# VectorE's order of work in the group loops of a graph network: the sums of a finished group are added ahead of the newest group's moments and roots

## What is computed

```
def _mlp(h, W1, b1, W2, b2, g, beta):
    h = silu(h @ W1 + b1)
    h = silu(h @ W2 + b2)
    return g * (h - mean(h)) * rsqrt(var(h) + 1e-5) + beta

edge_attr = _mlp(edge_attr, emb_...)                      # the embedding, edge_attr has 3 columns
for l in range(2):                                        # the two edge layers
    msg_in = concatenate([x[dst], x[src], edge_attr], 1)
    edges_new = _mlp(msg_in, e...[l]) + edge_attr
    agg = segment_sum(edges_new, dst, 3125)
    x = _mlp(concatenate([x, agg], 1), n...[l]) + x
    edge_attr = edges_new
```

## Time and profile before

| | |
|---|---|
| median of 3 runs | 4708.57 us (4707.64 to 4715.05) |
| the profiled execution's own time | 4716.08 us |
| its span | 4714.3 us |
| PE, PEld busy | 3298.3 us (70%), 2243.2 us (48%) |
| DVE busy | 2628.7 us (56%) |
| ACT busy | 1313.2 us (28%) |
| POOL busy | 2182.5 us (46%) |
| mean granted TensorE clock | 0.775 of 2.4 GHz |

### The profile page before, as it was taken

One profiled execution on the slowest core, in us unless ns is written; L12 is line 12 of the kernel. 1 busy time (PEld: TensorE's weight loads), 2 busy tenths in 40 slices (PEclk: granted clock), 3 DMA queues, 4 the chain that ended last, 5 costly groups with the idle time before them and its releaser, 6 DMA issues. The chain is left out here.

```text
span 4714.3 us, 78436 instructions
## 1 busy us (share of the span) xinstructions
PE 3298.3 (70%) x18717; PEld 2243.2 (48%) x18718; DVE 2628.7 (56%) x9408; ACT 1313.2 (28%) x2889; POOL 2182.5 (46%) x2147
## 2 busy tenths in 40 slices
PE   2477774566699999806999967999855555555553
PEld 1356653111466666504777745777633333333332
DVE  6666665677555544365888865767662222422222
ACT  0066663464011110002555533555430000000000
POOL 0577774000000000004777716777537777267774
PEclk7588886778799999957999978999965555655555
DMA  1222222000000000115666615444411111422223
GB/s 54 38 58 58 60 58 89 20 0 0 21 16 16 16 16 13 36 61 142 181 180 181 165 56 148 129 129 126 88 30 53 53 53 53 106 85 53 53 53 61
DMA packets 258206, 330.97 MB, mean 70 GB/s; under 512 B 79892, under 2 KB 170723, under 8 KB 256547
## 3 DMA queue, kind: packets, MB, share of 16 engines
q1 hardware_dynamic: 189372, 209.96, 14.6%
q0 software_dynamic: 68544, 117.46, 12.1%
HBM read 232.30 MB, written 94.47 MB: 69 GB/s over the span
## 5 line engine op out<-in xcount | busy, mean ns | idle before, releaser
L2246 PE MATMUL gat_acc<-gat_rows,gat_hot 128*128 128x128 f32 x1664 | 575.5, 478 | 487.0 <-issue 245.4
L908 PE MATMUL hop_p_a<-hop_h,adj 128*128 128x384 bf16 x4375 | 724.6, 328 | 26.8 <-DVE hop_h L849 26.8
L2246 PEld LDWEIGHTS gat_acc<-gat_rows,gat_hot 128*128 128x128 f32 x1664 | 400.9, 316 | 662.7 <-issue 661.7
L908 PEld LDWEIGHTS hop_p_a<-hop_h,adj 128*128 (+1 forms) x4375 | 429.3, 98 | 315.0 <-DVE hop_h L849 34.0
L1650 POOL DMA_INDIRECT la_far<-far_rows,la_idx x416 | 410.1, 986 | 295.4 <-DVE la_idx L1754 168.9
L1383 POOL DMA_INDIRECT by_src_records<-scatter_rec,scatter_rank x384 | 464.6, 1210 | 128.9 <-issue 115.5
L2230 POOL DMA_INDIRECT gat_rows<-typed_rows,gat_idx x416 | 394.9, 949 | 233.7 <-DVE gat_idx L2253 107.2
L1650 POOL DMA_INDIRECT lb_far<-far_rows,lb_idx x416 | 409.3, 984 | 196.9 <-issue 118.6
L2230 POOL DMA_INDIRECT gat_rows<-hidden_rows,gat_idx x416 | 395.2, 950 | 190.4 <-PE gat_acc L2246 80.1
L2261 DVE TENSOR_SCALAR gat_hot<-iota_row,gat_tabs 128x128 f32<-128x128 f32 x416 | 148.1, 366 | 369.8 <-PE gat_acc L2246 363.4
L520 POOL DMA_INDIRECT tabby_src_by_src_tab_rec<-by_src_records,by_src_off x4 | 4.0, 998 | 735.2 <-ACTq L595 734.2
(11 more groups left out here) (504 smaller groups left out, 6590.4 us busy)
## 6 DMA issues: line engine op xcount, KB each, us to landing
edge_features<-emb_out SPq DMA_DIRECT2D x104, 256.0 KB
la_feat<-edge_features SPq DMA_DIRECT2D x104, 256.0 KB, 3.0
edge_features<-la_out SPq DMA_DIRECT2D x104, 256.0 KB
lb_feat<-edge_features SPq DMA_DIRECT2D x104, 256.0 KB, 3.2
la_place<-dst_row SPq DMA_DIRECT2D x104, 128.0 KB
lb_place<-dst_row SPq DMA_DIRECT2D x104, 128.0 KB
typed_rows<-typed_np_row SPq DMA_DIRECT2D x25, 512.0 KB, 2.7
hop_side<-x0share_nodes SPq DMA_DIRECT2D x125, 64.0 KB, 1.8
```

Source lines behind the costliest of these rows:

```text
L908: ins = nc.tensor.matmul(p_a[(u.par + r) % 2][:, 0:3 * D], K.adj[:, s, bass.ds(u.t * P, P)], h3[r % 2][:, s, :, :].rearrange("p i d -> p ( ...
L2246: nc.tensor.matmul(acc[:, bass.ds(at[u % LOADS], D)], hot[u % HOTS][:, :], rows[u % RING][:, :], start=False, stop=True, skip_group_check= ...
```

## The change

On VectorE alone, in all three loops, the block that adds group g-OUT_LAG (with `outs` and, at each fourth group, the 16 register loads) moves from the end of turn g to its front, ahead of moments(g-1), hots, gathered moments, spreads and roots. In the embedding OUT_LAG is 8, in the edge layers 7. Nothing is added or taken out, and no other engine's program changes.

```diff
@@ embed_pass, VectorE
             for g in range(END):
+                q = g - OUT_LAG
+                if q >= 0:
+                    if q % BATCH == 0:
+                        at = tile_offsets(nc, mybir.EngineType.DVE, tile_row, q)
+                    add(q, at)
                 if 0 <= g - 1 < GE:
                     moments(nc, dve, ch, (s_s, s_stats), s, stats, mv, g - 1)
                 if 0 <= g - NORM_LAG < GE:
@@
                     if (g - 1) % BATCH == BATCH - 1 or g == GE:
                         roots(g - 1)
-                q = g - OUT_LAG
-                if q >= 0:
-                    if q % BATCH == 0:
-                        at = tile_offsets(nc, mybir.EngineType.DVE, tile_row, q)
-                    add(q, at)
@@ edge_pass, VectorE
                 if 8 <= g < 8 + 4 * NB and g % 4 == 0:
                     beta_share((g - 8) // 4)
+                q = g - OUT_LAG
+                if q >= 0:
+                    if keeps:
+                        outs(q)
+                    if q % BATCH == 0:
+                        at = tile_offsets(nc, mybir.EngineType.DVE, tile_row, q)
+                    add(q, at)
                 if 0 <= g - 1 < GE:
                     moments(nc, dve, ch, (s_s, s_stats), s, stats, mv, g - 1)
@@
                 if 0 <= g - 1 < GE and ((g - 1) % BATCH == BATCH - 1 or g == GE):
                     roots(g - 1)
-                q = g - OUT_LAG
-                if q >= 0:
-                    if keeps:
-                        outs(q)
-                    if q % BATCH == 0:
-                        at = tile_offsets(nc, mybir.EngineType.DVE, tile_row, q)
-                    add(q, at)
```

## The result

| | before | after |
|---|---|---|
| median of the runs taken together, us | 4711.06 (4 runs, 4707.64 to 4715.05) | 4669.90 (4 runs, 4666.28 to 4673.52) |
| profiled execution, us | 4716.08 | 4666.28 |
| its span, us | 4714.3 | 4664.5 |
| statistics of the embedding's loop, first and last start | 218.5, 731.7 | 217.2, 642.0 |
| scatters, first and last start | 192.0, 772.2 | 190.7, 778.0 |

The ratio is 0.9912, interval 0.9895 to 0.9929: 41 us less (33 to 49). Forecast were 4664 us and a gain of 44.6. The direction, the size and the mechanism held; several terms of the sum did not have their size.

A forecast was written before the change was run, and what follows sets the result against it. Edge loops were taken as bound by GpSimd's gathers, the embedding by VectorE and TensorE waiting in turn, with scatters as floor. 41 (embedding) + 3.6 (edges) = 44.6 off 4708.6 gives 4664 us, own range 4652 to 4676.

The forecast's parts named there:

- they set the end: Embedding's phase: with the loop shortened by 60 us, GpSimd's scatters, ending at 773.4, set the end, not the tail at 760.
- The discount for a group at 1.2 GHz: Embedding's loop: one slow TensorE group a batch returns 2.1 us, leaving 32 of 86 us gain; some 60 taken.
- rival (a): Embedding's loop gains only 32 us, short of the scatters' floor, through low clock behind remaining stalls: 4673 us; chance 0.18.
- The register loads: Embedding, VectorE: 16 loads a batch stay exposed at their new place, 1.27 us a batch.
- TensorE's remaining stall: Embedding's loop: TensorE still idles 4.4 us a batch waiting for hots, in two main pieces, 1.27 and 2.8 us.
- (c): Embedding's loop: short waits keep TensorE's granted clock at 0.50, 27 us more, total 4732 us; chance 0.04.
- The phase: Embedding: scatters' end 773.4 plus 3.5 collision and 2.6 landing; next phase at 781.5 instead of 822.5, gain 41 us.
- The collision priced from L690's row: Embedding's tail: L697 will run beside the scatters and lengthen one, as L690 did, by 0 to 3.5 us, taken at 3.5.
- The edges: Edge layers: loops stay with their gathers; only drains shorten, 2.1 us in layer 0 and 1.48 in layer 1, together 3.6.
- Rival (b): Gathers of both edge layers change length, 16 us either way: 4680 or 4648 us; chance 0.10.
- Their inputs are long there: Embedding: the moved adds need not wait, since TensorE's third of that group is a turn old.
- (d): Embedding: adds come no earlier because their own inputs are late, so TensorE's stall stays: 4709 us; chance 0.04.

The follow-up runs named there:

- e4: Changed kernel with six more of the 384 scatters issued in the phase before the embedding's (EARLY 22 instead of 16): 4666.17 us, ratio 0.9902.
- e5: Kernel before, old order, with the same six scatters issued in the phase before the embedding's: 4711.58 us, a single execution.
- e6: Changed kernel with two more bn_stats a group in the embedding, into a tile nobody reads: 4665.92 us, ratio 0.9901.
- e7: Changed kernel with layer 1's hots made twice, one into a tile nobody reads: 4688.47 us, a single execution.
- e9: Changed kernel with layer 1's hots reading their iota row from PSUM, on the slower occasion: 5269.96 us, ratio 1.0017.
- e2: Kernel before with the new order in the two edge layers alone, embedding as before: 4705.58 us, ratio 0.9988.
- e1: Kernel before with the new order in the embedding alone, edge layers as before: 4675.61 us, ratio 0.9929.
- e3: Kernel before with the embedding's adds moved ahead of the roots only, still behind moments and hots; edges as before: 4681.67 us, ratio 0.9934.
- e8: Changed kernel with layer 1's spread made twice, one into a tile nobody reads: 4664.90 us, a single execution.
- the last four runs: Changed kernel again, and three with layer 1's iota row in PSUM (two also with four scatters earlier), on a slower occasion: 5269.96 to 5297.05 us.
- e11: The changed kernel once more, unaltered, on the slower occasion: 5274.91 us, ratio 1.0040 to the kernel before beside it.

## Why the prediction was right, and where its terms were off

- **The floor.** The step "they set the end" is shown by e4, e5 and e6. This was the step that made the number; the loop alone would have given 88.
- **The loop.** Taken at some 60, at best 86, measured 88. VectorE's batch was forecast at 16.6 us and is 16.5, partly by luck: see the register loads. The discount for a group at 1.2 GHz was wrong: such stretches exist (clock 0.87 and not 1 over the loop), but ScalarE and TensorE run ahead and VectorE waits 18.9 us in all. The error cost nothing, since with either value the loop's tail ends before the scatters; but rival (a) thus got 0.18 that it did not deserve.
- **The register loads.** Counted at 1.27 us exposed a batch, and forecast to stay so. The batch above shows 0.48, and over the loop VectorE's adds idled 8.3 us in 14 places with the label issue, of 26 batches. That is 0.3 us a batch, 0.95 too few. The sum of 16.6 came right because waits that it left out took their place: 18.9 us for ScalarE's rows and 8.2 for TensorE's results ahead of the adds, 1.0 us a batch. Two errors cancelled.
- **TensorE's remaining stall.** Forecast in two pieces of at most 2.8 us, on the hots, 4.4 us a batch. The label fits, and the sign given (under 60 us on L1522) is met by more than asked, since that wait is gone. The size does not: 59.4 us are 2.3 a batch. TensorE was busy 362.65 of the 420 us, 14.2 a batch and not the 12.2 of the full clock, and that took the rest. The largest piece is 3.4 us, and behind it a slow stretch still follows (granted clock 0.50 from 516.5 to 522.5). (c), a clock that never comes back, did not happen: 0.87 against 0.82. The Trainium skill, "TensorE: Matmul & The Clock Gate", section "A second HAM failure mode: psum-queue depth-cycling", speaks for (a) or (c); the trace has the swings, and neither rival came true: VectorE's own 16.5 us a batch left room for them.
- **The phase.** Forecast from first scatter to L520 781.5 - 192.0 = 589.5 us, measured 594.6, so a gain of 36 instead of 41. Two terms were short. The scatters' row grew by 7.1 us (587.3 against 580.2 from first to last start) where I had 3.5: L697 took 4.50 - 1.18 = 3.3, and L829, which I had not looked at because the scatters were over when it ran, took 1.6; the rest is spread over many. And from the last scatter's end to L520 it is 785.28 - 779.16 = 6.1 us, not 2.6 + 2.0.
- **Rule or row.** The collision priced from L690's row came: L697 cost 3.3 us, and e7 and e9 show the same on the gathers. The Trainium skill, "SBUF — State Buffer", section "Who interferes with whom", infers that a two-input tensor_tensor leaves descriptor generation alone; by that L690, e7's copy and e9's PSUM operand would all have changed nothing. The rule beside it in that section, that an instruction with two SBUF inputs contends with a GpSimd instruction that reads SBUF, is not contradicted; no run here shows whether such a read is what is held up.
- **The edges.** Forecast 3.6 us, measured 5.8 in e2's median and 11 to 12 in the profiled executions of after and e2. The drains gave 4.3 us in layer 0 (40.1 to 35.8 from the last gather to the last add's start), where 2.1 were forecast, and 0.8 in layer 1, where 1.5 were. The other traces bear this out: layer 0's drain is 40.1 to 41.2 us in the four with the old order (before, e1, e3, e5) and 35.6 to 36.4 in the five with the new (after, e2, e4, e6, e8), layer 1's 33.4 to 33.7 and 32.0 to 32.6. That is about 6 us together, all of e2's 5.8. The rest of the 11 to 12 came from the gathers themselves (in the kernel after 1.9 and 4.1 us), which I had put at 0. The new order is not shown to be their cause: layer 1's gathers take 531.1 to 534.9 us with the old order and 528.9 to 532.4 with the new, and the ranges overlap. Rival (b), 16 us of it, did not come true.
- **The adds' inputs.** "Their inputs are long there" held in the embedding (8.2 us of waits in the loop). In layer 1 VectorE's adds now wait 66.4 us for TensorE's sums, where they had waited 2.0; it costs nothing, since that loop goes at the gathers' pace.
- **It does nothing.** (d) fell: no wait of TensorE on the adds is left. In the last four runs nothing was gained either; there the adds were not what TensorE waited for, and what set the pace is open.
- The median moved by 41.2, the profiled executions by 49.8; the former's lay 7.5 above the shown median before, and the latter's 3.6 below its own.

## What to carry to other kernels

When two engines wait for each other in turn, put the finished group's work ahead of any instruction that waits for new input; moving it past the long computation alone brought 35 of the loop's 88 us here. Before pricing it, look for what else ends the phase: once the loop was shorter than GpSimd's scatters, half of the gain was gone, and 43 us of added VectorE work cost nothing. List all large VectorE instructions that will come to run beside GpSimd's DMAs, not only the one that does so today.

## What was unexpected of the hardware

- A gather that starts while the hots or the spread are running ends 0.82 us behind them where that is later than its usual 0.94 us (43 lengthened gathers in layer 1 of the kernel after, within 0.01 us), and so takes up to 1.49 us instead of 0.94. The adds (one operand in PSUM) and the statistics do no such thing. With one of the hots' operands in PSUM the maximum falls from 1477 to 1065 ns; with the hots doubled the mean goes from 974 to 1010.
- Beside two-operand instructions of 3.5 to 3.9 us (L1539, L690, L697) a scatter ends some 1.05 us behind them and takes 3.2 to 4.7 us. In e9 and e11, where this work runs behind the last scatter, the longest of the 384 takes 1.23 and 1.56 us.
- L829, with one large operand (128 x 3584, 2.03 us), lengthened a scatter too, 2.79 us instead of 1.18, in each of three traces (after, e1, e3).
- The same program took 4.67 ms on one occasion and 5.27 ms on another, with all instructions but TensorE's as long as before and longer waits on transfers, and a 0.9% gain was not there in the second. The embedding's loop was slow only while GpSimd's scatters ran beside it, 6.8 us a group against 4.0 behind them.
